# Window attention on one core: scores in four 64x64 tiles, stacks moved without a stop in DRAM, and half of the f16 rounding on VectorE

## The chip, the cores and the metric

The kernel runs on one core of one Trainium2 chip. The metric is the device time of one execution in microseconds. Three runs of the kernel before gave 507.66, 511.57 and 513.79 us; the median is 511.57 us.

## The reference, cut to what matters

```python
# x: (8, 32, 32, 256) f32
x = x + L0(gn(x))        # 16 heads of 16 channels, windows of 8x8 = 64 tokens
x = x + L1(gn(x))        # gn: 32 groups of 8 channels over all pixels of a sample

# L0, for each of 8*16 windows
qkv = part @ qkv_w.T + qkv_b
attn = (q * SCALE) @ k.T + bias_table[REL_IDX] + MASK   # (windows, 16, 64, 64)
out = softmax(attn) @ v
# L1: h = x @ W.T + b, then over the 8 samples as time, for each pixel and channel
v = v + (h_t - v) / 2 ;  s = (v >= 1) ;  v = v * (1 - s)
```

L1 has a threshold, so L0 must be exact to almost f32. The kernel reaches that with operands split into two f16 parts, a rounded one ("hi") and the rest ("lo"), and with three products for each (hi hi, lo hi, hi lo).

## The kernel before, in words

The work is tiled by rows of windows: 8 samples of 4 rows of 4 windows, 32 rows in all. A row is two **pairs** of windows, so that the main loop has 64 pairs, `n` = 0 to 63; a pair is "even" (first of its row) or "odd". Each engine has its own instruction stream, written out by hand, in this order for every pair; the engines meet only at semaphores. No scheduler or planner reorders anything.

TensorE (`pair` at line 1076, the helpers above it), in the odd pair of row r: projections of q and k for row r + 2 (L934 to L936, 24 products); in the even pair: the projection of v for row r + 1 (L944 to L946, 12 products). Then `scores(n)`: for each of the two banks of `score_ps`, eight pairs of a bias product (L1007, full array) and a score product (L1011, 96 rows by 128 columns), 64 columns each. Between the banks it transposes the maxima of this pair (L1029, `turn_maxima`). It holds the last of the score products until `max_rows_done` and until the stacks for the next pair have landed (`await_tile_operands`, L1087), and then subtracts the maxima with 16 products in 64x64 tiles (L1021). Then come `max_scores` of the next pair (L982, L991), the products with v of the pair before (L1045, 24) and two transposes of the finished attention of n - 2 (L1055).

The score product takes its three f16 terms from **stacks**: 96 partitions, in which q_hi, q_lo and k_hi, k_lo stand above each other in the right order. A head's 16 channels lie spread over partitions in `q_flat` and `k_flat`, so the stacks are made by DMA. SyncE issues all of that on one queue (`move_q_and_k`, L318): 3 stores of the flat tiles to DRAM (L303, L306), then 12 loads from there (L309, L314), 15 transfers a row. `k_stack` is 128 columns wide with zeros where the other head is, so its loads write pieces of 64 f16. There are two stacks each, used by turns.

ScalarE, for every pair: (odd) normalisation of row r + 3 (L481) and the rounded parts of q and k (L503); (even) `xn_hi` (L497) and the rounded v (L520); the transposed maxima (L599); then for each bank the exponential twice, once in f32 (`probs`, L608) and once rounded to f16 (`p_hi`, L609); and the bias of the attention (L572).

GpSimd: `p_lo = probs - p_hi` for each bank (L446, waits for `p_hi_done`), the addition of the attention to x (L432), `xn_lo` (L402) and once a sample the Newton steps of the norm (L225 to L233), whose result ScalarE needs for the normalisation (L481).

VectorE: the low parts of q, k (L758) and v (L777), the maxima (L783), statistics (L647), the division of the attention (L794, L798), and the small steps of the norm (L676 to L690).

Setup ahead of the loop splits the weights (L543, L732), scales the biases (L737, L739), and makes four variants of the position bias plus mask (L751, L528, L532, L418), the last two of them beside pairs 3 and 4. The spiking stage (L874 to L883, L923) comes after pair 63 and takes the last 70 us or so.

Of the kernel before, what the change touches and what calls it, by code (L numbers as in the profile page):

```python
# [6 lines left out]
def swin_attention_then_lif_kernel(nc, image, x, qkv_w, qkv_b, bias_table, lif_w, lif_b, out):  # L7
# [14 lines left out]
    ALU = mybir.AluOpType  # L22
# [25 lines left out]
    with ctx:  # L48
# [16 lines left out]
        both_parts = sb("both_parts", [128, 2, WS], f16)  # L65
        group_avg = sb("group_avg", [128, 128], f32)
        pick_max = sb("pick_max", [128, 2 * HALVES, 128], f16)
        bias_k = sb("bias_k", [128, 4, 2 * QUADS, 128], f16)
        bias_q = sb("bias_q", [128, 4, 2, HALVES, 128], f16)
# [24 lines left out]
        k_stack = [sb(f"k_stack{i}", [128, QUADS, HALVES * WCOLS, 128], f16) for i in range(2)]  # L94
        q_spill = [nc.dram_tensor(f"q_spill{i}", [2, 32, QUADS, HALVES * ROWTOK], f16).ap() for i in range(2)]
        k_spill = [[nc.dram_tensor(f"k_spill{i}{part}", [32, QUADS, HALVES * ROWTOK], f16).ap() for part in ("hi", "lo")] for i in range(2)]
# [26 lines left out]
        stack_cleared = sem("stack_cleared")  # L123
# [30 lines left out]
        q_spilled = sem("q_spilled")  # L154
        k_hi_spilled = sem("k_hi_spilled")
        k_lo_spilled = sem("k_lo_spilled")
# [8 lines left out]
        p_hi_done = sem("p_hi_done")  # L165
# [30 lines left out]
        def slot_total(row, y, per):  # L196

            return (row + (2 - y % 2)) * (per // 2)
# [57 lines left out]
        def w_columns(tile, first, c, h, ordered):  # L256

            cols = tile[:, c, first + h * 128:first + (h + 1) * 128]
            if first == 2 * C:
                return cols  # L260
            if ordered:
                return cols.rearrange("p (r g) -> p r g", g=QUADS)
            return cols.rearrange("p (g r) -> p r g", g=QUADS)
# [22 lines left out]
        def _(sp):  # L286
# [15 lines left out]
            def spill(flat, part, spilled, kept):  # L302
                sp.dma_start(kept.rearrange("r g n -> (r g) n"), flat[:, part, :]).then_inc(spilled, 16)  # L303

            def spill_q(slot):
                sp.dma_start(q_spill[slot].rearrange("t r g n -> (r g) t n"), q_flat[:, :, :]).then_inc(q_spilled, 16)  # L306

            def stack_q(slot, rows, kept):
                sp.dma_start(q_stack[slot][rows, :, :, :].rearrange("r g n i -> r (g n i)"), kept).then_inc(stacked[slot], 16)  # L309
# [327 lines left out]
        def _(dve):  # L637
# [182 lines left out]
            def pair(n, row, k, s):  # L820
# [11 lines left out]
                if not is_last_pair(n):  # L832
                    maxima(n + 1)
# [331 lines left out]
```

## Time and profile before

| | us |
|---|---|
| median of 3 runs | 511.57 |
| the profiled execution's own time | 516.01 |
| its span, first to last instruction | 514.3 |
| TensorE busy | 433.2 (84%) |
| VectorE busy | 408.8 (79%) |
| ScalarE busy | 380.1 (74%) |
| GpSimd busy | 274.8 (53%) |
| mean granted TensorE clock | 0.950 of full |
| DMA: packets, under 512 bytes | 136780, 107506 |

No engine is busy all the time; TensorE is nearest to it, but its busy time is that of modelled, pipelined matmuls. The chain that ended last gives 19% of the span to the queue of SyncE, 31% to TensorE, 13% to ScalarE and 11% to DMA.

### The profile page before, as it was taken

Reading aid. Unit: us, or ns where it says so; the run is one execution under the profiler, and the core shown is the slowest. Engines: PE = TensorE matmul, PEld = TensorE weight load, DVE = VectorE, ACT = ScalarE, POOL = GpSimd, SP = SyncE. Lnnn points to the kernel's source line nnn. Section 1 sums busy time; section 2 is a strip of 40 time slices with the busy share of each in tenths; the row PEclk is TensorE's granted clock in tenths of the full one; section 3 lists DMA queues with packets and bytes.
Section 4 is the critical chain, followed back from the end, with each engine's and each line's share of the span. In section 5 each row is a group of like instructions: output and inputs, shape, how many; then the busy total and the mean of one; then the engine's idle time right before and its main releaser. Section 6 shows DMA issues by size and latency. Waiting matters only on the chain.

```text
span 514.3 us, 19277 instructions
## 1 busy us (share of the span) xinstructions
PE 433.2 (84%) x7848; PEld 400.7 (78%) x7848; DVE 408.8 (79%) x872; ACT 380.1 (74%) x897; POOL 274.8 (53%) x380
## 2 busy tenths in 40 slices
PE   0477956998889879889988898989898987799996
PEld 0366856987889879789878797978798986588885
DVE  7957866798789859868888778879767887588887
ACT  6357776887889869779878787978788957745560
POOL 3534674567566746567666557556756648420000
PEclk9977977999999989989999989999999989889999
DMA  7145551465555563565555555554545450023333
GB/s 216 70 104 144 126 123 47 101 149 134 126 123 136 125 151 83 144 151 130 111 147 127 135 135 132 130 135 104 112 104 116 107 138 13 22 103 124 143 128 139
DMA packets 136780, 61.56 MB, mean 120 GB/s; under 512 B 107506, under 2 KB 125172, under 8 KB 136692
## 3 DMA queue, kind: packets, MB, share of 16 engines
q1 hardware_dynamic: 136352, 60.33, 46.5%
q8 instruction: 62, 1.02, 0.9%
q14 instruction: 26, 0.21, 0.1%
q10 hardware_dynamic: 340, 0.01, 0.0%
HBM read 35.13 MB, written 25.17 MB: 117 GB/s over the span
## 4 chain that ended last, share of the span: by engine, by line
PE 31%; SPq 19%; ACT 13%; DMA 11%; DVE 10%; issue 7%; POOL 7%; ACTq 0%; DVEq 0%; POOLq 0%
SPq L314 13%; DMA k_stack<-k_spill0lo 5%; SPq L309 4%; PE pv_ps L1045 3%; POOL p_lo L446 3%; PE score_ps L923 3%; ACT v_hi L520 3%; PE proj_ps L923 3%; PE pv_ps L923 3%; DMA k_stack<-k_spill1lo 2%; PE proj_ps L934 2%; PE score_ps L1021 2%; ACT k_flat L503 2%; PE max_ps L923 2%; PE proj_ps L935 2%
## 5 line engine op out<-in xcount | busy, mean ns | idle before, releaser
L446 POOL TENSOR_TENSOR p_lo<-probs,p_hi 128x512 f16<-128x512 f32 x128 | 146.4, 1165 | 132.7 <-ACT p_hi L609 78.9
L1011 PE MATMUL score_ps<-q_stack,k_stack 96*128 96x64 f16 x1024 | 86.6, 194 | 45.2 <-ACT max_rows L599 18.0
L1011 PEld LDWEIGHTS score_ps<-q_stack,k_stack 96*128 96x128 f16 x1024 | 71.9, 98 | 52.5 <-ACT max_rows L599 38.5
L608 ACT ACTIVATE probs<-score_ps 128x512 f32<-128x512 f32 x128 | 77.0, 602 | 46.9 <-PE score_ps L1021 43.4
L783 DVE TENSOR_REDUCE neg_max<-max_ps 128x16 f16<-128x1024 f32 x64 | 78.3, 1224 | 27.6 <-PE max_ps L991 26.6
L934 PE MATMUL proj_ps<-xn_hi,w_hi 128*128 128x256 f32 x256 | 78.6, 307 | 12.7 <-DVE w_lo L732 8.1
L1007 PE MATMUL score_ps<-both_parts,bias_k 128*128 128x64 f16 x1024 | 78.3, 194 | 0.0
L609 ACT ACTIVATE p_hi<-score_ps 128x512 f16<-128x512 f32 x128 | 77.4, 605 | 0.0
L777 DVE TENSOR_TENSOR v_lo<-proj_ps,v_hi 64x256 f16<-64x256 f32 x128 | 54.2, 424 | 28.4 <-ACT v_hi L520 26.8
L935 PE MATMUL proj_ps<-xn_lo,w_hi 128*128 128x256 f32 x256 | 74.1, 289 | 0.0
L936 PE MATMUL proj_ps<-xn_hi,w_lo 128*128 128x256 f32 x256 | 73.8, 288 | 0.0
L1007 PEld LDWEIGHTS score_ps<-both_parts,bias_k 128*128 128x128 f16 x1024 | 70.5, 99 | 2.7
L934 PEld LDWEIGHTS proj_ps<-xn_hi,w_hi 128*128 128x128 f32 x256 | 51.0, 199 | 16.6 <-DVE w_lo L732 8.1
L1045 PE MATMUL pv_ps<-v_hi,p_hi 128*128 128x68 f16 x512 | 57.7, 200 | 2.8 <-POOL p_lo L446 2.8
L520 ACT ACTIVATE v_hi<-proj_ps 64x256 f16<-64x256 f32 x128 | 50.4, 394 | 13.0 <-PE proj_ps L946 11.5
L1045 PE MATMUL pv_ps<-v_lo,p_hi 128*128 128x68 f16 x512 | 57.5, 198 | 0.0
L1045 PE MATMUL pv_ps<-v_hi,p_lo 128*128 128x68 f16 x512 | 57.3, 198 | 0.0
L798 DVE TENSOR_TENSOR attn<-pv_ps,recip 64x256 f32<-64x256 f32 x128 | 54.0, 422 | 3.0
L1045 PEld LDWEIGHTS pv_ps<-v_hi,p_hi 128*128 128x128 f16 x512 | 50.1, 102 | 8.0 <-POOL p_lo L446 3.4
L935 PEld LDWEIGHTS proj_ps<-xn_lo,w_hi 128*128 128x128 f32 x256 | 51.1, 199 | 0.0
L936 PEld LDWEIGHTS proj_ps<-xn_hi,w_lo 128*128 128x128 f32 x256 | 50.9, 199 | 0.0
L1045 PEld LDWEIGHTS pv_ps<-v_hi,p_lo 128*128 128x128 f16 x512 | 50.0, 100 | 0.0
(130 smaller groups left out, 1214.2 us busy)
## 6 DMA issues: line engine op xcount, KB each, us to landing
xc<-in_x_dram SPq DMA_DIRECT2D x32, 256.0 KB, 3.5
q_spill<-q_flat SPq DMA_DIRECT2D x32, 256.0 KB, 2.7
q_stack<-q_spill SPq DMA_DIRECT2D x32, 256.0 KB, 3.7
out_dram<-xc SPq DMA_DIRECT2D x32, 256.0 KB, 2.3
q_stack<-q_spill SPq DMA_DIRECT2D x32, 128.0 KB, 3.8
k_spill0hi<-k_flat SPq DMA_DIRECT2D x16, 128.0 KB, 2.2
k_spill0lo<-k_flat SPq DMA_DIRECT2D x16, 128.0 KB, 3.3
k_stack<-k_spill0hi SPq DMA_DIRECT2D x32, 64.0 KB, 3.1
```

The lines of the kernel that those rows point to most:

```text
L314: sp.dma_start(k_stack[slot][rows, quads, :, e * WS:(e + 1) * WS], k_spill[slot][part][e * D:(e + 1) * D, quads, :].rearrange("d g (n j) - ...
L446: pool.tensor_tensor(p_lo[p][:, quads, :, :].rearrange("p g w i -> p (g w i)"), probs[:, quads, :, :].rearrange("p g w i -> p (g w i)"), p ...
L520: last = act.activation(v_block(v_hi[slot], w, e), v_part(w, e), ACT.Copy)
L608: act.activation(probs[:, quads, :, :].rearrange("p g w i -> p (g w i)"), score_ps[:, h, :], ACT.Exp)
L609: act.activation(p_hi[p][:, quads, :, :].rearrange("p g w i -> p (g w i)"), score_ps[:, h, :], ACT.Exp)\
L783: dve.tensor_reduce(neg_max[:, :].rearrange("p (m n) -> p m n", m=2)[:, :, 0:8], max_ps[:, :, :].rearrange("p m (n j) -> p m n j", j=WS), ...
L934: pe.matmul(dst, w_hi[:, c, cols], high[:, tok], start=(c == 0), stop=False)
L935: pe.matmul(dst, w_hi[:, c, cols], low[:, tok], start=False, stop=False)
L936: last = pe.matmul(dst, w_lo[:, c, cols], high[:, tok], start=False, stop=(c == HALVES - 1))
L1007: pe.matmul(dst, bias_k[:, variant(k, w), h * QUADS + 2 * mid + q, :], both_parts[:, 0, :], start=(h == 0 and q == 0 and w == 0), stop=False)
L1011: pe.matmul(dst, k_stack[slot][0:96, 2 * mid + q, at, :], q_stack[slot][0:96, 2 * mid + q, at, :], start=False, stop=False)
L1045: last = pe.matmul(cols[:, :, g, :], pp[p][:, g // 2 * 4 + h * 2 + g % 2, :, :].rearrange("p w i -> p (w i)"), vv[k // 2][:, p, h * QUADS ...
```

## The change

Four things are done together.

1. **Scores.** The score products and the bias products go in four 64x64 tiles of the array. The stacks are 48 partitions high and come twice, at partitions 0 and 64; `k_stack` has no zeros and is half as wide. For a pair there are now 32 score products of 64 columns (L1007 of the new kernel) and 8 bias products of 512 columns (L1016) in place of 16 and 16 on the full array; `max_scores` has 4 bias products of 512 and 32 tile products of 64 columns in place of 8 of 256 and 16 of 128; the transpose of the maxima becomes 4 products in tiles, written in f32. Both banks are now begun only after ScalarE has read both banks of the pair before (`exp_done`), and the maxima are turned ahead of the products, not between the banks. The wait for the next stacks stands ahead of `max_scores`.
2. **Stacks.** They are filled straight from `q_flat` and `k_flat`, 12 transfers a row with 64 KB each in pieces of 1 KB, and none through DRAM. All 12 wait for `score_ps_done` of the odd pair that frees the slot. The four writers of the flat tiles (L503 on ScalarE, L758 on VectorE in the kernel before) now wait until all 12 transfers of the row before have landed (`await_moved`).
3. **Rounding.** For the first bank ScalarE computes the exponential once; VectorE rounds it to f16 after the maxima (L832), and GpSimd's first `p_lo` waits for that.
4. **Setup.** No clearing of the stacks; the scaling of the biases goes ahead of the norm's first roots; the weights are put in another order of columns; the bias variants are written in eight smaller steps on ScalarE and four on GpSimd.

```diff
             def move_q_and_k(slot, r):
 
-                sp.wait_ge(k_hi_done, r + 1)
-                spill(k_flat, HI, k_hi_spilled, k_spill[slot][0])
-                sp.wait_ge(k_lo_done, r + 1)
-                spill_q(slot)
+                sp.wait_ge(q_flat_done, r + 1)
                 if not is_first(r, 2):
                     sp.wait_ge(score_ps_done, 4 * (r - 2) + 4)
-                spill(k_flat, LO, k_lo_spilled, k_spill[slot][1])
-                sp.wait_ge(k_hi_spilled, (r + 1) * 16)
-                stack_k(slot, 0, 0, slice(0, QUADS))
-                stack_k(slot, 32, 0, slice(0, 2))
-                stack_k(slot, 64, 0, slice(2, QUADS))
-                sp.wait_ge(q_spilled, (r + 1) * 16)
...
+                stack(slot, q_stack, 0, q_flat, HI)
+                stack(slot, q_stack, 2, q_flat, HI)
+                sp.wait_ge(k_hi_done, r + 1)
+                stack(slot, k_stack, 0, k_flat, HI)
+                stack(slot, k_stack, 1, k_flat, HI)
+                sp.wait_ge(q_lo_done, r + 1)
+                stack(slot, q_stack, 1, q_flat, LO)
+                sp.wait_ge(k_lo_done, r + 1)
+                stack(slot, k_stack, 2, k_flat, LO)
...
+            def stack(slot, stacks, term, flat, part):
+                for r in range(2):
+                    first = r * WS + term * D
+                    sp.dma_start(stacks[slot][first:first + D, :, :, :].rearrange("d g n i -> d g (n i)"),
+                                 flat[r * WS:(r + 1) * WS, part, :])\
                       .then_inc(stacked[slot], 16)
...
+        def await_moved(eng, r):
+
+            if r > 0:
+                eng.wait_ge(stacked[(r - 1) % 2], stacked_total(r - 1))
...
             def q_high(done):
                 act.wait_ge(q_ps_done, done)
-                wait(act, q_spilled, 16 * (done - 1))
+                await_moved(act, done - 1)
                 with_bias(q_flat, 0).then_inc(q_flat_done, 1)
...
-                    act.activation(probs[:, quads, :, :].rearrange("p g w i -> p (g w i)"), score_ps[:, h, :], ACT.Exp)
-                    act.activation(p_hi[p][:, quads, :, :].rearrange("p g w i -> p (g w i)"), score_ps[:, h, :], ACT.Exp)\
-                       .then_inc(p_hi_done, 1)
+                    last = act.activation(probs[:, quads, :, :].rearrange("p g w i -> p (g w i)"), score_ps[:, h, :], ACT.Exp)
+                    if h == 1:
+                        last = act.activation(p_hi[p][:, quads, :, :].rearrange("p g w i -> p (g w i)"), score_ps[:, h, :], ACT.Exp)
+                    last.then_inc(exp_done, 1)
...
                 if not is_last_pair(n):
                     maxima(n + 1)
+                wait(dve, pv_ps_done, n - 1)
+                dve.wait_ge(exp_done, n * 2 + 1)
+                dve.tensor_copy(p_hi[p][:, 0:QUADS, :, :].rearrange("p g w i -> p (g w i)"),
+                                probs[:, 0:QUADS, :, :].rearrange("p g w i -> p (g w i)")).then_inc(p_hi_copied, 1)
...
+            def scores(n, row, k):
 
                 slot, p = k // 2 % 2, k % 2
...
+                for g, w in itertools.product(range(QUADS), range(2)):
+                    col = (2 * g + w) * WS
+                    for h, e in itertools.product(range(HALVES), range(2)):
+                        at = h * WCOLS + 2 * p + w
+                        rows = stacks_of[e ^ h]
+                        pe.matmul(score_ps[halves[e], h, col:col + WS], k_stack[slot][rows, g, at, :], q_stack[slot][rows, g, at, :],
+                                  start=(g == 0 and w == 0), stop=False)
...
+                        pe.matmul(score_ps[halves[e], h, :].rearrange("p (g w i) -> p g w i", g=QUADS, w=2), flip[rows, :], biases,
+                                  start=False, stop=False)
+                pe.wait_ge(max_rows_done, n + 1)
...
-                scores(n, row, k, await_tile_operands)
+                wait(pe, exp_done, n * 2)
+                turn_maxima(n)
+                scores(n, row, k)
...
                 if not is_last_pair(n):
+                    await_max_operands(*following)
                     max_scores(following[2])
```

How the change moves instructions, at three places. First TensorE, around `scores` of pair 0: the end of it before (-; fifteen more pairs of L1007 and L1011 stand ahead), and all of it now (+), with `max_scores` of pair 0 ahead and of pair 1 behind.

```order
-L1011 MATMUL score_ps<-q_stack,k_stack 128x64
-L1021 MATMUL score_ps<-max_rows,pick_max 64x2x64 x16
-L982 MATMUL max_ps<-bias_q,ident_h 64x256 x8
-L991 MATMUL max_ps<-k_stack,q_stack 64x128 x16
+L987 MATMUL max_ps<-bias_q,ident_h 64x512 x4
+L994 MATMUL max_ps<-k_stack,q_stack 64x64 x32
+L1033 MATMUL max_ps<-ident_h,neg_max 64x64 x4
+L1007 MATMUL score_ps<-q_stack,k_stack 64x64 x32
+L1016 MATMUL score_ps<-bias_s,flip 64x512 x8
+L1023 MATMUL score_ps<-max_rows,pick_max 64x2x64 x16
+L987 MATMUL max_ps<-bias_q,ident_h 64x512 x4
+L994 MATMUL max_ps<-k_stack,q_stack 64x64 x32
```

The turn of the maxima (L1033) now stands ahead of all score products, and nothing but the 16 products L1023 stands behind the wait for ScalarE's `max_rows`.

Second, SyncE's queue, the transfers of one row. Before:

```order
L303 DMA k_spill1hi<-k_flat 128x512 [waits k_hi_done]
L306 DMA q_spill<-q_flat 128x2x512 [waits k_lo_done]
L303 DMA k_spill1lo<-k_flat 128x512 [waits score_ps_done]
L314 DMA k_stack<-k_spill1hi 16x32x64 [waits k_hi_spilled]
L314 DMA k_stack<-k_spill1hi 16x32x64
L314 DMA k_stack<-k_spill1hi 16x16x64 x4
L309 DMA q_stack<-q_spill 64x2048 [waits q_spilled]
L309 DMA q_stack<-q_spill 32x2048
L314 DMA k_stack<-k_spill1lo 16x16x64 [waits k_lo_spilled]
L314 DMA k_stack<-k_spill1lo 16x16x64 x3
```

And now:

```order
L310 DMA q_stack<-q_flat 16x4x512 [waits score_ps_done,q_flat_done]
L310 DMA q_stack<-q_flat 16x4x512 x3
L310 DMA k_stack<-k_flat 16x4x512 [waits k_hi_done]
L310 DMA k_stack<-k_flat 16x4x512 x3
L310 DMA q_stack<-q_flat 16x4x512 [waits q_lo_done]
L310 DMA q_stack<-q_flat 16x4x512
L310 DMA k_stack<-k_flat 16x4x512 [waits k_lo_done]
L310 DMA k_stack<-k_flat 16x4x512
```

Fifteen transfers in two steps have become twelve in one, but the first of them now waits for `score_ps_done`, which before only the third did.

Third, VectorE in a plain even pair and the odd one behind it, now; before, the two CAST rows were not there and the rest was the same.

```order
L779 TENSOR_REDUCE neg_max<-max_ps 128x2x8
L832 CAST p_hi<-probs 128x512
L790 RECIPROCAL recip<-pv_ps 128x32
L794 TENSOR_TENSOR attn<-pv_ps,recip 64x256 x2
L641 BN_STATS x_stats<-xc 128x6 x2
L754 SCALAR_TENSOR_TENSOR q_flat<-proj_ps,b_cols,q_flat 128x256 x2
L754 SCALAR_TENSOR_TENSOR k_flat<-proj_ps,b_cols,k_flat 128x256 x2
L779 TENSOR_REDUCE neg_max<-max_ps 128x2x8
L832 CAST p_hi<-probs 128x512
L641 BN_STATS x_stats<-xc 128x6 x2
```

The rounding stands right behind the maxima of the next pair, and whatever VectorE does after it comes later by its length.

## Rows read from the trace of the kernel before

**Rows 1.** Waits over the whole execution: engine, line, releaser; us, times, longest.
```profile
PE score_ps L1011 <- DMA k_stack<-k_spill0lo: 15.2, 11, 2.0
PE score_ps L1011 <- DMA k_stack<-k_spill1lo: 9.9, 8, 2.7
ACT xn L481 <- POOL shift L233: 8.8, 7, 1.4
```

**Rows 2.** Chain that ended last, in order of time: start, length, what.
```profile
225.26 0.21 PE proj_ps L944
...
231.07 0.12 PE proj_ps L934
```

**Rows 3.** Windows of 1 us: busy by engine (instructions), clock, DMA share, GB/s.
```profile
187.00:188.00 1.00, 1.00 (x6) 1.00 (x6) 1.00 (x4) 1.00 (x4) 1.00 (x1) 0.50 0.33 52
```

**Rows 4.** ScalarE in order of time: start, length, line, operation, count [idle before].
```profile
98.47 0.28 ACT L599 ACTIVATE max_rows<-max_ps 128x128 f16<-128x128 f16 x1
...
228.64 0.28 ACT L599 ACTIVATE max_rows<-max_ps 128x128 f16<-128x128 f16 x1
...
234.11 0.84 ACT L503 ACTIVATE k_flat<-proj_ps,b_cols 128x256 f16<-128x256 f32 x2
234.84 0.28 ACT L599 ACTIVATE max_rows<-max_ps 128x128 f16<-128x128 f16 x1
235.84 0.60 ACT L608 ACTIVATE probs<-score_ps 128x512 f32<-128x512 f32 x1 [0.72 <-PE score_ps L1021]
236.33 0.59 ACT L609 ACTIVATE p_hi<-score_ps 128x512 f16<-128x512 f32 x1
...
239.60 0.28 ACT L599 ACTIVATE max_rows<-max_ps 128x128 f16<-128x128 f16 x1
...
243.65 0.87 ACT L503 ACTIVATE q_flat<-proj_ps,b_cols 128x256 f16<-128x256 f32 x2
...
415.31 0.28 ACT L599 ACTIVATE max_rows<-max_ps 128x128 f16<-128x128 f16 x1
```

**Rows 5.** TensorE in order of time, from the last score product to max_scores.
```profile
228.97 0.20 PE L1011 MATMUL score_ps<-q_stack,k_stack 96*128 96x64 f16 x1
229.10 0.42 PE L1021 MATMUL score_ps<-max_rows,pick_max 64*64 64x128 f16 x16
229.35 0.39 PE L982 MATMUL max_ps<-bias_q,ident_h 64*64 64x256 f16 x8
229.57 0.39 PE L991 MATMUL max_ps<-k_stack,q_stack 64*64 64x128 f16 x16
```

**Rows 6.** SyncE's queue in order of time.
```profile
236.82 3.39 SPq L314 DMA_DIRECT2D k_stack<-k_spill0hi  x6
...
256.34 0.92 SPq L347 DMA_DIRECT2D xc<-in_x_dram  x2
```

**Rows 7.** DMA issues of the page: count, KB each, median us from issue to landing.
```profile
k_spill1hi<-k_flat SPq DMA_DIRECT2D x16, 128.0 KB, 1.7
...
k_stack<-k_spill1lo SPq DMA_DIRECT2D x64, 32.0 KB, 3.1
```

**Rows 8.** VectorE in order of time, setup and one odd pair.
```profile
10.20 0.86 DVE L724 COPY pick_max<-ident_h 64x512 f16<-64x512 f16 x2
...
13.90 4.17 DVE L732 SCALAR_TENSOR_TENSOR w_lo<-w_raw,w_hi 128x128 fp32r<-128x128 f32 x12
17.99 5.02 DVE L737 TENSOR_SCALAR b_cols<-b_cols 128x2 f32<-128x2 f32 x1
...
236.22 1.23 DVE L783 TENSOR_REDUCE neg_max<-max_ps 128x16 f16<-128x1024 f32 x1 [0.36 <-PE max_ps L991]
```

**Rows 9.** GpSimd in order of time, setup.
```profile
20.09 2.89 POOL L382 MEMSET v_lo<- 128x1088 f16 x3
```

**Rows 10.** Chain that ended last, setup and last pairs.
```profile
26.31 0.58 PE proj_ps L944
...
439.93 2.28 POOL p_lo L446 x2
```

More of the change, by code:

```diff
@@ L640, in _ @@
             dve.memset(three_halves[:, :], 1.5)
-            for slot in range(2):
-                dve.memset(q_stack[slot][96:128, 2:QUADS, :, :].rearrange("r g n i -> r (g n i)").bitcast(f32), 0.0)
             dve.memset(masks[:, :, :], 0.0).then_inc(setup_dve, 1)
@@ L985, in max_scores @@
-                for w in range(2):
-                    for h in range(HALVES):
-                        col = (2 * w + h) * 128
-                        at = h * WCOLS + 2 * (k % 2) + w
-                        for mid, rows in enumerate(halves):
-                            for q, queries in enumerate(halves):
-                                last = pe.matmul(max_ps[queries, mid, col:col + 128], q_stack[slot][rows, 2 * mid + q, at, :],
-                                                 k_stack[slot][rows, 2 * mid + q, at, :],
-                                                 start=False, stop=(w == 1 and h == 1))
+                first, last_variant = variant(k, 0), variant(k, 1)
@@ new lines, in scores @@
+                pe.wait_ge(max_rows_done, n + 1)
+                for w, m in itertools.product(range(2), range(2)):
+                    for h, e in itertools.product(range(HALVES), range(2)):
+                        rows = halves[e ^ h]
+                        dst = score_ps[halves[e], h, :].rearrange("p (m q w i) -> p m w q i", m=2, q=2, w=2)[:, m, w, :, :]
+                        last = pe.matmul(dst, pick_max[rows, (2 * w + m) * 2 + h, :],
+                                         max_rows[p][rows, :].rearrange("p (q i) -> p q i", q=2),
+                                         start=False, stop=(w == 1 and m == 1))
+                        if w == 1 and m == 1 and e == 1:
+                            last.then_inc(score_ps_done, 1)
@@ L1027, in turn_maxima @@
             def turn_maxima(n):
                 pe.wait_ge(neg_max_done, n + 1)
-                pe.transpose(max_ps[:, 0, :].bitcast(f16)[:, 0:128], neg_max[:, :], ident_h[:, :])\
-                  .then_inc(max_turned, 1)
+                for q, queries in enumerate(halves):
+                    for rows in halves:
+                        last = pe.matmul(max_ps[rows, q, 0:WS], neg_max[queries, rows], ident_h[queries, queries], start=True, stop=True)
+                last.then_inc(max_turned, 1)
```

202 lines of the change are left out of this document (88 added, 114 removed).

## Prediction

> **What bounds the kernel now.** I read the table of waits first, since no engine is busy all the time. TensorE waits 25.1 us (15.2 + 9.9, 19 times) for the transfers that fill the stacks [rows 1]; nothing else that a transfer does holds an engine so long. Then the chain that ended last, which says what a wait costs behind it: after a long one, v's projection runs at 0.21 us a product [rows 2], because the granted clock is 0.50, the lower of the two levels, 1.2 GHz, for some 3.5 us [rows 3]; undisturbed it takes 0.12 us [rows 2]. Then ScalarE in order of time, because its `max_rows` comes once a pair and marks the beat. From pair 7 to pair 59 it beats from 98.47 to 415.31 us [rows 4], 26 rows of windows in 316.84 us, 12.19 us a row. Where no transfer is late, a row takes 10.96 us: 6.20 from the even pair to the odd (228.64 to 234.84), 4.76 from there to the next (to 239.60) [rows 4]. So the stacks cost about 1 us a row, and the rest is a beat in which TensorE and ScalarE hand work to each other.
>
> **The sum**, against the profiled execution's own 516.0 us.
>
> *Stack waits.* The stacks no longer go through DRAM: one landing (1.7 to 3.1 us [rows 7]) and three issues fewer. I take all 25.1 us of waits away, but give back 0.26 us for each of the 19, the gap in which TensorE waits for `max_rows` anyway (4.9 us), and add four stretches at half clock, 12 v products each, at 0.09 us (0.21 - 0.12 [rows 2]), 1.1 us: 4.3. That is **-24.5**.
>
> *TensorE's products.* The tile products before pass at 16 of 128 columns in 0.22 us and 8 of 256 in 0.22 us (229.35 to 229.57, and as much again) [rows 5], so four tiles work at once. The 32 products of 64 columns then take 0.22 us if columns set the pace and at most 0.44 if every instruction costs what L991's do. `max_scores` goes from 0.44 to 0.43 to 0.65 us and stands on the path; I take +0.1. In `scores` 1 us of full-array work becomes 0.22 to 0.44 + 0.43 us (8 of 512 columns at twice L982's time), but that is hidden: from the end of k's projection (234.11) ScalarE still needs to 235.12 for `k_flat` and `max_rows` [rows 4]. What stood on the path there is the last score product ahead of L1021, 0.13 us (228.97 to 229.10 [rows 5]), and it goes. Over 62 pairs (0.1 - 0.13): **-2**. The Trainium skill (TensorEngine Tiling (Array Packing), Performance Considerations, Instruction Overhead) speaks against small tiles: each matmul has about 60 cycles of overhead, so that few columns save nothing. By that rule 64 columns are just long enough to be worth issuing, and the sum would stay as it is; no row here has a product of 64 columns in a tile.
>
> *ScalarE's exponential.* One of four goes; the step from one to the next is 0.49 us (235.84 to 236.33 [rows 4]), 31 us in all. I count **0**: k's rounding at 234.11 begins when TensorE's projection ends, and the v rounding of the even pair likewise, so ScalarE would wait there instead.
>
> *VectorE's rounding.* 64 new casts of 512 elements. COPY of 512 took 0.43 us each (0.86 for 2 [rows 8]); at the pace of L783, 1.23 us for 1024 [rows 8], it would be about 0.7. I take 0.43, since the form is nearest. It stands behind the maxima, 0.38 + 1.14 us after the exponentials start (236.22 against 235.84, and its length [rows 4, 8]), so GpSimd's first `p_lo` starts 2.0 us after them, where it now can at 1.2: 0.8 us later. Mostly hidden: TensorE wants `p_lo` only after the next `scores`, 4.8 us on. Not hidden where GpSimd is the chain: seven times, once a sample, ScalarE waits 8.8 us in all for its roots [rows 1], and 0.85 more each is **+6**. And in the last pairs, with no projection left to cover, `p_lo` is on the chain that ended last [rows 10]: three times 0.8, **+2.5**.
>
> *The new wait `await_moved`.* Twelve issues at 0.46 us (0.92 for two [rows 6]), the last landing 2.2 us after its issue (between 1.7 and 3.1 [rows 7]), begun 0.1 us after the odd pair's score products: the move ends 7.8 us after them. The next `q_flat` starts 7.81 us after the exponentials in a fast row (243.65 against 235.84 [rows 4]). So it just fits. Behind it VectorE gets tight: busy 79% of the span, about 9.6 of 12.19 us a row, it will have 10.5 of some 11.5. What both give back by coming late now and then I put at 0.2 us for 29 rows, an estimate: **+5**. Bounds for the move: 12 x 0.46 + 1.7 = 7.2 us, which costs nothing, and 12 x 0.57 (3.39 for six [rows 6]) + 3.1 = 10 us, which is rival A.
>
> *Setup.* `b_cols` stands 5.02 us on VectorE [rows 8], while GpSimd clears v (its memsets run to 22.98 [rows 9]), and v's projection starts only at 26.31 [rows 10]. Now that scaling comes before GpSimd is busy, and v can follow k's projection at 23.2: **-3**. It is -3 only if the bias sum L751 that moves up isn't held by the same memsets; L732, with two inputs as well, ended at 18.07 [rows 8] with the first three memsets under way (17.2, as the other three start at 20.09 [rows 9]). If it is held, 0. The Trainium skill agrees (SBUF — State Buffer, SBUF: two separate sides): VectorE and GpSimd share a pair of ports under a lock, and an operation with two SBUF inputs meets it only against a GpSimd operation that reads SBUF. The bias variants are written in more and smaller steps: **+2**.
>
> Sum: -24.5 - 2 + 0 + 6 + 2.5 + 5 - 3 + 2 = **-14**, 502 us against 516.0. The median of the runs lies 4.4 us under the profiled execution; late transfers are what differs from one to the next, and these are what goes, so I give half of that: **499.5 us**, 2.4% under the median. 1% of the median (506.5 to 516.7) is about what a measurement can tell from no change.
>
> **Rivals.**
>
> A. *The queue becomes the loop* (slower). If the moves take 0.57 us an issue and 3.1 to land, they end 10 us after the odd scores; then comes what is left of a fast row behind `q_flat`, 10.96 - 7.81 = 3.15 us, so a row takes 13.2 us, 1.0 over today's 12.19: 29 us on 516, less 3 to 5 of setup and of the runs' median, about **540**. It decides from a move of 9.0 us on. For it: all 12 transfers now wait for the odd scores, and ScalarE itself waits for their landing, which it did not. Against it: the pieces are of 1 KB, where 107506 of 136780 packets were under 512 bytes, and the 0.57 us belong to transfers cut into the smallest. 9%.
>
> B. *The tiles run two at a time, not four* (slower). `score_ps` bank 0 is now written by both halves of rows, partitions 0 to 63 from one and 64 to 127 from the other; before, each bank had one row half. At half rate the bias and score products take 0.86 + 0.44 to 0.88 us and the 16 of L1021 (0.25 us [rows 5]) twice that: 0.25 + about 0.45 beyond ScalarE's cover of 1.0 us, 0.7 x 62 = 43 us more, about **542**. The Trainium skill has such a rule (TensorEngine Tiling (Array Packing), Restrictions and Gotchas, PSUM Pressure): different row tiles cannot access the same PSUM bank simultaneously. Against it: no partition of a bank is written from two row halves at a time. 6%.
>
> C. *VectorE fills the row* (no change). With casts of 0.7 us, now and then held by an operation of GpSimd, it has 11.0 to 11.2 us of work in 11.5 and cannot catch up behind a wait; it gives back 0.4 us more a row: 499.5 + 12, **511**. 18%.
>
> D. *The freed time is used* (faster). ScalarE's half microsecond shortens the step from odd to even, and the last transfers' jitter is gone: 10.7 us a row where I count on 11.5, half of that in the 26 rows: **489**. 12%.
>
> E. The stacks come too late again from somewhere else, so that the change does not do what it says, and the time stays at 512. 3%.
>
> My forecast has the rest, 52%, with 491 to 508 as its own range. With D, most of C and E the range is **486 to 518**; A, B and the edges lie outside. Faster by over 1%: 0.60 (most of the forecast, and D); within 1%: 0.24 (its upper end, C and E); slower: 0.16 (A, B).
>
> **What would show it.** TensorE's waits for `k_stack` and `q_stack` near nothing, and no stretch at clock 0.50 in the main loop. `max_rows` 11.0 to 11.5 us a row, and one row a sample near 13, ScalarE waiting 2 us for GpSimd's roots there. 32 products of 64 columns in 0.2 to 0.45 us. The cast at 0.43 us, GpSimd's first `p_lo` 2 us behind the exponentials. ScalarE's `q_flat` with little or no wait for a transfer: waits of 1 us there are rival A. v's first projection at 23 us and not at 26.31. I am wrong if rows stay at 12 us with the stack waits gone; then the loop has closed over another engine, and VectorE's idle time in a row says whether it is C.

## The result and the profile after

| | median us | runs | ratio to before | span of the profile | clock |
|---|---|---|---|---|---|
| before, beside it | 511.87 | 4 (507.66 to 513.79) | 1 | 514.3 | |
| changed | 565.15 | 4 (562.96 to 566.6) | 1.105 [1.0972, 1.1127] | 563.1 | 0.915 |

The change makes the kernel 10.5% slower; I had forecast 499.5 us and a range of 486 to 518. The page of the changed kernel: busy time and share, DMA, and the chain that ended last by engine.

```profile
span 563.1 us, 22270 instructions
PE 432.4 (77%) x9320; PEld 368.5 (65%) x9320; DVE 431.6 (77%) x936; ACT 354.3 (63%) x849; POOL 282.3 (50%) x392
DMA packets 42488, 44.98 MB, mean 80 GB/s; under 512 B 8082, under 2 KB 33940, under 8 KB 42388
SPq 31%; PE 21%; ACT 13%; DMA 11%; DVE 9%; POOL 7%; issue 7%; ACTq 0%; DVEq 0%; POOLq 0%
```

TensorE has as much work as before, in a longer span. There is a third as many packets, and yet SyncE's queue has grown from 19% of the chain to 31%. The waits of the changed kernel (engine, line, releaser: us, times, longest):

```profile
POOL p_lo L439 <- DVE p_hi L832: 181.7, 55, 6.3
PEld score_ps L1023 <- ACT max_rows L594: 117.1, 63, 6.7
ACT q_flat L500 <- DMA k_stack<-k_flat: 56.8, 25, 4.4
DVE q_flat L754 <- ACT q_flat L500: 45.0, 25, 3.7
ACT xn L478 <- POOL shift L233: 18.0, 7, 3.5
```

TensorE's 25.1 us of waits for the stacks [rows 1] are gone, as forecast: no wait of TensorE for a transfer is left. ScalarE now waits 56.8 us for the transfers that fill the stacks, 25 times, ahead of `q_flat`; and its seven waits for the roots grew from 8.8 us [rows 1] to 18.0. The beat, which answers to [rows 4] (ScalarE: start, length, instruction [idle before]):

```profile
102.64 0.29 ACT L594 ACTIVATE max_rows<-max_ps 128x128 f16<-128x128 f32 x1
...
243.64 1.09 ACT L603 ACTIVATE probs<-score_ps 128x512 f32<-128x512 f32 x2 [0.81 <-PE score_ps L1023]
...
254.50 0.84 ACT L500 ACTIVATE q_flat<-proj_ps,b_cols 128x256 f16<-128x256 f32 x2 [1.04 <-DMA k_stack<-k_flat]
...
256.43 0.29 ACT L594 ACTIVATE max_rows<-max_ps 128x128 f16<-128x128 f32 x1
257.31 1.08 ACT L603 ACTIVATE probs<-score_ps 128x512 f32<-128x512 f32 x2 [0.59 <-PE score_ps L1023]
...
462.20 0.29 ACT L594 ACTIVATE max_rows<-max_ps 128x128 f16<-128x128 f32 x1
```

Pair 7 to pair 59 takes 359.56 us, 13.83 a row against 12.19. These 26 rows hold 42.7 of the 48.8 us between the two spans. The rest: first `max_rows` 1.1 us earlier (42.12 against 43.24), from there to pair 7 5.3 more, from pair 59 to the last pair 2.9 more, and after it 1.0 less. Why a row takes 13.8 us is in the chain of waits from one odd pair's scores to the next row's `q_flat` (start, length, what):

```profile
242.88 0.70 PE score_ps L1023 x16
...
243.64 0.55 SPq L310
...
246.14 1.54 SPq L310
...
247.72 0.59 SPq L310
...
250.91 0.60 SPq L310
...
251.55 2.86 DMA k_stack<-k_flat
...
254.50 0.10 ACT q_flat L500
```

The scores end at 243.58, eleven issues at 251.51, and the twelfth, begun at 251.55, has landed at 254.41 (2.86 us from its issue). Then `q_flat`, k's flat, `max_rows` and the next odd scores follow, to 257.25, and SyncE starts again at 257.31. This is a closed ring of 13.67 us: odd scores, twelve issues one behind the other, landing, `q_flat`, odd scores. Each step waits for the one before it. It closes in the mean of the 26 rows too: 0.13 us to the first issue, 8.21 from there to the start of the twelfth, 2.79 to `q_flat`, 2.71 to the end of the next odd scores, together the 13.83 of the row.

TensorE is idle for most of the time ahead of the odd scores, and behind that its granted clock is at the lower of its two levels, 1.2 GHz (window: busy by engine with instructions, clock, DMA share, GB/s). In the ring this costs some 0.2 us: the 16 products of the odd scores take 0.70 us at 242.88 and 0.47 in the next row.

```profile
241.00:243.00 2.00, 0.12 (x8) 0.12 (x11) 1.18 (x3) 1.83 (x6) 1.25 (x2) 0.80 0.00 0
243.00:248.00 5.00, 5.00 (x87) 4.69 (x88) 3.89 (x9) 2.72 (x6) 1.86 (x2) 0.50 0.18 56
```

### The profile page after: what moved, and what is told of

It is laid out like the page before. It is cut to its first block, busy times and chain, and to the rows that moved or that the text cites. A ratio compares the mean times of both kernels' runs of the same rounds, so it can differ in the third digit from the quotient of the medians.

```text
span 563.1 us, 22270 instructions
## 1 busy us (share of the span) xinstructions
PE 432.4 (77%) x9320; PEld 368.5 (65%) x9320; DVE 431.6 (77%) x936; ACT 354.3 (63%) x849; POOL 282.3 (50%) x392
## 4 chain that ended last, share of the span: by engine, by line
SPq 31%; PE 21%; ACT 13%; DMA 11%; DVE 9%; POOL 7%; issue 7%; ACTq 0%; DVEq 0%; POOLq 0%
SPq L310 30%; DMA k_stack<-k_flat 10%; ACT k_flat L500 3%; ACT q_flat L500 3%; ACT xn L478 3%; PE score_ps L1023 3%; PE proj_ps L923 2%; PE pv_ps L923 2%; PE score_ps L923 2%; POOL p_lo L439 2%; PE max_ps L923 2%; PE pv_ps L1049 2%; ACT v_hi L517 2%; POOL xn_lo L391 2%; ACT max_rows L594 1%
## 5 line engine op out<-in xcount | busy, mean ns | idle before, releaser
L1023 PE MATMUL score_ps<-max_rows,pick_max 64*64 64x128 f16 x1024 | 28.7, 234 | 86.4 <-ACT max_rows L594 86.3
L1023 PEld LDWEIGHTS score_ps<-max_rows,pick_max 64*64 64x64 f16 x1024 | 17.8, 112 | 117.3 <-ACT max_rows L594 117.1
L934 PE MATMUL proj_ps<-xn_hi,w_hi 128*128 128x256 f32 x256 | 77.7, 303 | 18.0 <-POOL xn_lo L391 13.8
L603 ACT ACTIVATE probs<-score_ps 128x512 f32<-128x512 f32 x128 | 69.7, 595 | 26.7 <-PE score_ps L1023 20.4
L1049 PE MATMUL pv_ps<-v_hi,p_hi 128*128 128x68 f16 x512 | 63.7, 208 | 5.1 <-POOL p_lo L439 4.8
L500 ACT ACTIVATE q_flat<-proj_ps,b_cols 128x256 f16<-128x256 f32 x64 | 26.8, 469 | 64.0 <-DMA k_stack<-k_flat 56.8
L1049 PE MATMUL pv_ps<-v_lo,p_hi 128*128 128x68 f16 x512 | 63.8, 207 | 0.0
L1049 PE MATMUL pv_ps<-v_hi,p_lo 128*128 128x68 f16 x512 | 63.7, 207 | 0.0
L754 DVE SCALAR_TENSOR_TENSOR q_flat<-proj_ps,b_cols,q_flat 128x256 f16<-128x256 f32 x64 | 28.0, 479 | 45.2 <-ACT q_flat L500 45.0
L567 ACT ACTIVATE attn_cm<-proj_ps,b_cols 128x128 f32<-128x128 f32 x128 | 40.4, 371 | 22.7 <-PE proj_ps L1059 22.7
L1049 PEld LDWEIGHTS pv_ps<-v_lo,p_hi 128*128 128x128 f16 x512 | 53.0, 107 | 0.3
```

What stands on the lines that cost most here:

```text
L500: last = act.activation(flat[:, HI, tok], proj_ps[:, first // 2, tok], ACT.Identity, bias=b_cols[:, first + h:first + h + 1])
L603: last = act.activation(probs[:, quads, :, :].rearrange("p g w i -> p (g w i)"), score_ps[:, h, :], ACT.Exp)
L934: pe.matmul(dst, w_hi[:, c, cols], high[:, tok], start=(c == 0), stop=False)
L1023: last = pe.matmul(dst, pick_max[rows, (2 * w + m) * 2 + h, :], max_rows[p][rows, :].rearrange("p (q i) -> p q i", q=2), start=False, stop ...
L1049: last = pe.matmul(cols[:, :, g, :], pp[p][:, h * QUADS + g, :, :].rearrange("p w i -> p (w i)"), vv[k // 2][:, p, h * QUADS + g, :, :, :] ...
```

## The experiments

Ratios are to the kernel before, measured beside each, with 95% intervals. "e5", in the second group, is the version that beats both kernels.

| | kernel | median us | ratio |
|---|---|---|---|
| e1 | changed, two flat tiles | 519.75 | 1.0138 [1.0079, 1.0197] |
| e2 | changed, three slots | 526.82 | 1.0271 [1.0204, 1.0338] |
| e3 | changed, both | 517.59 | 1.0107 [1.0076, 1.0138] |
| e4 | changed, ScalarE rounds | 563.35 | 1.0945 [1.0845, 1.1045] |
| e5 | e3, ScalarE rounds | 487.41 | 0.9643 [0.9557, 0.9729] |
| e6 | before, VectorE rounds | 531.64 | 1.0417 [1.0141, 1.0694] |
| e7 | e3, rounding ahead of the maxima | 498.42 | 0.987 [0.9792, 0.9947] |
| e8 | changed, 14 transfers | 607.63 | 1.2008 [1.192, 1.2096] |
| e9 | before, three slots | 512.54 | 0.9951 [0.9913, 0.9989] |
| e10 | e5 without the third slot | 496.9 | 0.9656 [0.9584, 0.9728] |
| e11 | e5 without the second flat tiles | 513.76 | 0.9982 [0.9938, 1.0025] |
| e12 | e5, seven single transfers in three rows | 527.99, one run | |
| e13 | e5 and an idle rounding | 511.65 | 1.0005 [0.9959, 1.0052] |
| e14 | e5, xn_hi behind max_rows | 502.47 | 0.9818 [0.9754, 0.9882] |
| e15 | e5 again | 485.53 | 0.9493 [0.9435, 0.9551] |
| e16 | e5, VectorE's wait alone | 486.74 | 0.9508 [0.9412, 0.9603] |
| e17 | e16 and 0.52 us of load | 488.96 | 0.9542 [0.9468, 0.9616] |
| e18 | e17 and p_lo held by it | 519.98 | 1.0148 [1.0064, 1.0231] |

### The ring: e1, e2, e3, e8

The ring has two edges that buffers can cut: q_flat waits for the landing (a second flat tile), and the first issue waits for the odd scores (a third slot).

```diff
-        q_flat = sb("q_flat", [128, 2, HALVES * ROWTOK], f16)
+        q_flat = [sb(f"q_flat{i}", [128, 2, HALVES * ROWTOK], f16) for i in range(2)]   # e1, e3; k_flat alike
...
-                await_moved(act, done - 1)
+                await_moved(act, done - 2)
...
-                    sp.wait_ge(score_ps_done, 4 * (r - 2) + 4)
+                    sp.wait_ge(score_ps_done, 4 * (r - 3) + 4)                          # e2, e3; slots row % 3
```

> The changed kernel with two flat tiles each for q and k, used by turns, so that their writers wait for the move of two rows back and not for the last one. Theory R (a ring of the queue: odd scores, 12 issues of 0.63 us, landing, the wait before q's rounding, next odd scores): the waits of ScalarE for a transfer (56.8 us over 25 rows) go, the row falls from 13.8 to some 11.2 us, and the time to about 500 us. Theory V (VectorE's rounding makes p_lo late, GpSimd waits 181.7 us for it, and that sets the row): nothing changes, 560 us or more. Theory T (the products in tiles and the clock are what costs): 560 us too.

> The changed kernel with three stacks each and not two, so that a move no longer waits for the odd pair's scores; the wait of the flat tiles' writers for the last move stays. Theory R: the move starts when q's rounded part is there, about 2.5 us earlier, and the ring closes over q's rounding alone: 12 issues, landing, q's rounding, 10.9 us or a little more; row near 11.5, time 505 to 515 us. Theories V and T: 560 us.

> Both of the edits before in one. Theory R: no ring is left, only the queue's own load of 12 issues a row (8.3 us of 11): as e1 or a few us less, 490 to 500 us. If the queue's load itself were the bound it would stay near e1. Theories V and T: 560 us.

Cutting either edge takes 38 to 45 us away, both 47.6. That is nearly all of the loss of 53.3 us, and it is the ring. With one edge cut something is left at the other: in e1 TensorE's products wait 2.7 us for the stacks (its weight loads, at the same places, 4.3), in e2 `q_flat` on ScalarE waits 28.6 us; in e3 no engine waits for a stack's transfer. But all three are 12 to 20 us slower than I had expected from the ring alone, and e3 still isn't faster than before. The group on the rounding looks for that rest.

e8 lengthens the ring instead:

```diff
+                for r2 in range(2):
+                    sp.dma_start(spare[r2 * D:(r2 + 1) * D, :, :], q_flat[r2 * WS:(r2 + 1) * WS, HI, :]).then_inc(stacked[slot], 16)
```

> The changed kernel with two more transfers of the same shape per row, to a spare tile that nobody reads (14 instead of 12 in the move). Theory R (the ring: exponential, q_flat, issues one after the other, landing of the last, next q_flat): each row pays 2 x 0.63 = 1.26 us, 26 to 29 rows, 565 goes to 597 to 602. Rival (the landing and bandwidth, not the issue, sets the ring): the last landing shifts by less, 565 to 580.

The time goes up 42 us, the row from 13.83 to 15.19. That is 1.36 us for two transfers, 0.68 each: the median issue (0.59 + 0.04) and a little more, as nearly every move has a long issue in it (below). It is somewhat above the 597 to 602 expected; the direction and the size fit the ring.

### The rounding: e4 to e7

```diff
-                    if h == 1:
+                    if True:                      # ScalarE rounds both banks: e4 on the changed kernel, e5 on e3
                         last = act.activation(p_hi[p][:, quads, :, :]..., ACT.Exp)
...
-                dve.wait_ge(exp_done, n * 2 + 1)
-                dve.tensor_copy(p_hi[p][:, 0:QUADS, :, :]..., probs[:, 0:QUADS, :, :]...).then_inc(p_hi_copied, 1)
```

> The changed kernel with ScalarE taking the exponential of the first bank twice again, and no rounding on VectorE. Theory R: ScalarE has waits to spare in the ring, so nothing but the once-a-sample wait for GpSimd's roots gets shorter, 0.8 us seven times: 555 to 562 us. Theory V: the loss goes, 515 us or less.

> Two q_flat/k_flat tiles and three slots as in e3, and ScalarE rounds both banks again. Theory G (with the ring gone, the rounding on VectorE is what is left: it starts behind the maxima of the next pair, so the GpSimd subtraction p_lo, the xn_lo behind it and project_q come about 1 us later in each row, and 1.7 us later in the rows with the roots): row 12.20 goes to about 11.6 and the time to 498 to 504. Rival S (SyncE's twelve issues at 0.62 us, 7.4 us of queue in each row plus their landing, are what is left, and ScalarE gets its 0.60 us a pair back on the path): 515 to 530.

Within the ring it makes no difference who rounds (e4, 563.35 against 565.15), since the rest waits for the queue anyway. With the ring open it makes 30 us (e3 517.59, e5 487.41), more than the 14 to 20 that I had expected. Whoever had tried e4 alone would have acquitted the rounding.

e6 adds VectorE's rounding to the kernel before, e7 moves it ahead of the maxima in e3:

> The kernel before with one thing of the change: VectorE rounds the first bank, behind the maxima, and ScalarE only the second. Prices part three alone. Theory G: GpSimd's chain is as late here as in e3, so 517 to 526. Rival (the delay is hidden behind the 9.4 us waits for the stacks through the spill): 508 to 514. My prediction put +8.5 on the rounding and nothing back from ScalarE: 520.

> e3 with VectorE's rounding put ahead of the maxima of the next pair (in the trace of e3 the exponential of the first bank ends at 241.4 and the rounding starts at 243.02, behind the 1.23 us reduction). Theory G: p_lo starts 1 us earlier, row 12.20 to 11.8 or so, 505 to 512. Rival M: the maxima come 0.4 us later or wait for the exponential, the turn and the next scores with them, and what GpSimd gains TensorE loses: 516 to 525.

e6: +4.2%, some 18 us, with a wide interval (its four runs took 523.8 to 533.5 us); three of the four lie above the 517 to 526 of theory G. e7: 498.42, 19 us below e3 and 11 above e5, below what either side expected. So the place of the rounding in VectorE's order is most of its price. The chain of e3 in one row shows the way it takes (start, length, what):

```profile
239.35 1.11 POOL p_lo L439
240.46 0.69 POOL xc L422
241.15 1.24 POOL xn_lo L391
...
242.44 0.39 PE proj_ps L934
...
245.57 0.84 ACT k_flat L500 x2
...
246.63 0.42 PE score_ps L1023 x16
247.05 0.22 PE max_ps L987 x4
247.26 0.24 PE max_ps L994 x29
```

GpSimd runs `p_lo`, the residual's sum and `xn_lo` without a gap, and q's projection starts when `xn_lo` is done. In e5 `xn_lo` ends 0.5 us ahead of q's projection (GpSimd, then TensorE, in order of time):

```profile
225.83 2.29 POOL L436 TENSOR_TENSOR p_lo<-probs,p_hi 128x512 f16<-128x512 f32 x2 [2.90 <-PE pv_ps L1042]
228.08 0.73 POOL L422 TENSOR_TENSOR xc<-xc,attn_cm 128x256 f32<-128x256 f32 x1
228.76 1.28 POOL L391 TENSOR_TENSOR xn_lo<-xn,xn_hi 128x512 fp32r<-128x512 f32 x1
```

```profile
230.54 0.36 PE L927 MATMUL proj_ps<-xn_hi,w_hi 128*128 128x256 f32 x1
```

So I had the right engine and the wrong cover. I had counted on TensorE wanting `p_lo` 4.8 us later; what matters in this row is `xn_lo`, two places behind `p_lo` in GpSimd's queue. In the rows with roots it is the Newton steps, which stand behind `xn_lo` and which ScalarE's normalisation waits for, in e3 (first row) and in e5:

```profile
ACT xn L478 <- POOL shift L233: 23.0, 7, 3.5
```

```profile
ACT xn L475 <- POOL shift L233: 7.0, 6, 1.3
```

### What of the rounding costs: e13, e16, e17, e18

> e5 with VectorE's rounding added at the place it has in the change (behind the maxima), into a spare tile that nobody reads; ScalarE rounds both banks too, and GpSimd waits for ScalarE. Theory G (what costs is that the subtraction p_lo waits for VectorE): 487 to 493, VectorE's 0.43 us a pair is absorbed. Rival L (VectorE's load, or its hold on GpSimd while it rounds, is what costs): 500 to 518, as in e3.

e13 gave 511.65, as if VectorE's load cost 26 us. But its rounding isn't the change's. In e3 (first row) GpSimd waits for it; in e13 (the other two, VectorE and GpSimd) it meets `p_lo`:

```profile
243.02 0.43 DVE L832 CAST p_hi<-probs 128x512 f16<-128x512 f32 x1
```

```profile
292.64 1.38 DVE L832 CAST spare<-probs 128x512 f16<-128x512 f32 x1
...
291.44 2.30 POOL L437 TENSOR_TENSOR p_lo<-probs,p_hi 128x512 f16<-128x512 f32 x2 [0.73 <-ACT p_hi L605]
```

0.43 us alone, 1.38 beside `p_lo`; the median of e13's 63 is 1.10 us, where the changed kernel's 64 have 0.43, and VectorE is busy 88% of the span. The Trainium skill (SBUF — State Buffer, SBUF: two separate sides) has such a rule: a VectorE operation in a two-port mode or with two SBUF inputs and a GpSimd operation share one pair of ports under an exclusive lock, and who comes second waits for the whole instruction of the other. The trace agrees: the rounding starts at 292.64 while the second `p_lo` runs, until 293.74, and ends 0.28 us behind it; 61 of the 63 end 0.2 to 0.35 us behind the GpSimd instruction in which they began. No row says in which mode the rounding runs. How the 26 us divide between VectorE's longer time and operations of GpSimd held by it wasn't tried. The next three leave that out, with a reduction from one source:

```diff
+                dve.wait_ge(exp_done, n * 2 + 1)                                                       # e16, e17, e18
+                dve.tensor_reduce(spare[:, :], w_hi[:, 0, 0:352].bitcast(f32), AX.X, ALU.max)          # e17, e18 (.then_inc(p_hi_copied, 1))
...
+                        pool.wait_ge(p_hi_copied, n + 1)                                               # e18, ahead of the first p_lo
```

> e5, and VectorE waits behind the maxima for the first bank's exponential, with no instruction of its own. Theory G (the lateness of p_lo costs): 485 to 489. Rival W (VectorE's queue held for the exponential costs): 495 or more.

> e16 with a reduction of 352 constants per partition behind the wait, about 0.43 us of VectorE in each pair, that shares nothing with GpSimd. Theory G: 487 to 494. Rival L (VectorE's load): 500 or more.

> e17 with GpSimd's first p_lo held until that reduction is done, as the change holds it for the rounding; ScalarE still rounds both banks. Theory G: the step from e17 to here is most of the 30 us, 508 to 520. Rival: within 5 us of e17, and what is left is ScalarE's order in the change.

486.7, 489.0, 520.0. VectorE's wait costs nothing that can be measured (e15, e5 again, is 485.5), its load 2 us (the reduction takes 0.515 us, a little more than the rounding's 0.43), and `p_lo` held until VectorE is through 31 us. e18's row is 12.18 us, e3's 12.20. This settles it: the lateness of `p_lo` is the price, and the load is not. Most of it is paid in few rows: from pair 7 to pair 59 e18 takes 26.0 us longer than e17, 17.9 of them in the six rows with roots (15.2 us each against 12.2), the other 8.1 in twenty rows.

### What is left, and why the direct move pays: e9 to e12, e14, e15

> The kernel before, moves through DRAM and all, with nothing changed but a third slot for both stacks and for the spill, so that a row's move starts a row earlier. Theory B (the 24.5 us of waits for the stacks are a matter of buffers, and the direct move is not needed to be rid of them): 485 to 500, and of the 26 us that e5 gains on the kernel before the direct move and the tiles hold little. Rival D (the gain of e5 is the direct move's and the tiles'): 505 to 514.

Theory B is refuted: 0.5% is all that a third slot gives the kernel before (its third slot found room only once two tiles of the last stage were laid over the bias table). 21.9 of the 25.1 us of waits for the stacks stay. SyncE in e9, and the wait that TensorE has for the move before:

```profile
230.78 0.63 SPq L303 DMA_DIRECT2D k_spill1hi<-k_flat  x1
...
233.22 3.36 SPq L314 DMA_DIRECT2D k_stack<-k_spill1hi  x6
236.62 1.85 SPq L309 DMA_DIRECT2D q_stack<-q_spill  x2
238.52 1.90 SPq L314 DMA_DIRECT2D k_stack<-k_spill1lo  x4
243.31 0.34 SPq L303 DMA_DIRECT2D k_spill2hi<-k_flat  x1
```

```profile
232.56 0.19 PE L1012 MATMUL score_ps<-q_stack,k_stack 96*128 96x64 f16 x1 [1.62 <-DMA k_stack<-k_spill0lo]
```

The move starts with k's flat and not with a free slot, its last issue ends 9.6 us later, and a landing comes on top (in the median row of e9 it is 12.2 us from the first issue to the last landing): the way through DRAM is by itself as long as the row that it has, 12.07 us. The direct move is shorter (10.77 us in the row above, 243.64 to 254.41). That this is what it buys, once it may overlap the row, is argued from these lengths; no run has the direct move without the tiles.

```diff
# e10 = e5 without three slots, e11 = e5 without two flat tiles, e5's rounding in both
```

> e5 without the third slot: two q_flat/k_flat tiles, ScalarE rounds both banks. Theory R (the ring has two edges, odd scores to the first issue and last landing to q_flat; cutting either opens it): within 1% of e5, 487 to 493. Rival (the third slot is what starts the move early enough, and the second flat tile only shifts the wait to TensorE): 500 to 520.

> e5 without the second flat tiles: three slots, ScalarE rounds both banks. Theory R: the ring is cut at its other edge, but q_flat still waits for a landing; the move takes 10.8 us of a row of 10.8 to 11.2 us, so it is just too long: 495 to 510. Rival: as good as e5, 487 to 492.

The second flat tile is the edge to cut: 0.9656, where e5 had 0.9643. In microseconds it is 496.9 against 487.4, outside the 487 to 493 expected, in a row of 11.77 us against 11.22; and in e10 TensorE's products still wait 7.6 us for the stacks, ten times, where in e5 none does. So the third slot may be worth a few us on top; the ratios don't settle it. The third slot alone leaves `q_flat` waiting for landings, 26.3 us in 20 waits, a row of 12.22 us: the time of before, 0.9982, worse than I expected of theory R.

```diff
+                    for dst, what in ((spare[0:64, 0, :], src[0:64]), (spare[:, 0, :], src), (spare[0:32, :, :], src), (spare_dram, src), ...):
+                        sp.dma_start(dst, what).then_inc(spare_sem, 16)
+                        sp.wait_ge(spare_sem, 16 * spare_count[0])
```

> e5 with seven single transfers behind the moves of rows 4, 12 and 20, each waited for before the next: 64x1 KB to 64 partitions, 128x1 KB to 128 partitions, 128x1 KB to 32 partitions of 4 KB, 128x1 KB to DRAM, 16x1 KB, 64x1 KB to 16 partitions of 4 KB (the shape of the stacks' moves), 128x256 B. Theory I (an issue's time goes with its rows): 64x1 KB 0.59 us in either layout, 128 rows 1.0 or more, 16 rows below 0.4. Rival (a fixed price per transfer inside the chip's memory, lower to DRAM: 0.46 us in the spills of the kernel before): 0.59 for all of them but the one to DRAM, 0.46. The time itself tells nothing here, SyncE waits on purpose.

SyncE's issues behind the move of row 4, in the order of the expectation (start, length); from issue to landing they took 1.93, 2.03, 2.76, 1.78, 1.81, 2.37 and 2.05 us by the chain:

```profile
95.20 0.51 SPq L342 DMA_DIRECT2D spare<-w_hi  x1
97.14 0.51 SPq L342 DMA_DIRECT2D spare<-w_hi  x1
99.19 0.60 SPq L342 DMA_DIRECT2D spare<-w_hi  x1
101.97 0.34 SPq L342 DMA_DIRECT2D spare_dram<-w_hi  x1
103.77 0.60 SPq L342 DMA_DIRECT2D spare<-w_hi  x1
105.60 0.59 SPq L342 DMA_DIRECT2D spare<-w_hi  x1
107.99 0.51 SPq L342 DMA_DIRECT2D spare<-w_hi  x1
```

Neither theory holds. Among these seven an issue doesn't go with rows or bytes: 16 rows of 1 KB 0.60, 128 rows 0.51. It goes with where it writes: DRAM 0.34, SBUF over 64 or 128 partitions 0.50 to 0.51, over 16 or 32 partitions 0.58 to 0.61, and so again in rows 12 and 20. The stacks' moves are of the dearest kind. (This one execution took 527.99 us, which says nothing: SyncE waits for each landing.) But that is no rule for all transfers. In the kernel before, by the medians of their places in the row, the loads from DRAM into 16 partitions of `k_stack` take 0.55 and 0.63 us with 64 KB, and with 32 KB 0.42 to 0.45 in seven places and 0.62 in one; two stores of one shape to DRAM take 0.338 and 0.466. So the destination isn't all, and e12 doesn't say what else there is.

```diff
-                    xn_high(k // 2 % 2, row + 3)        # ahead of max_rows
+                    xn_high(k // 2 % 2, row + 3)        # behind it
```

> e5 with xn_hi put behind the copy of the maxima (max_rows) on ScalarE instead of ahead of it. In e5's chain of waits, from 226.53 on, attn_cm 0.65, xn_hi 0.52 and half of v_hi 0.63 stand between the exponentials and max_rows at 228.37. Theory A (ScalarE's order sets the even beat): 0.5 us less in each row, 26 to 29 rows, 473 to 479. Rival X (xn_lo and project_q, 0.7 us later than now, take it back in the odd beat): 484 to 490.

Refuted: 502.47, 17 us slower than e5 beside it (e15) and slower than the rival said as well. The step from odd to even stays at 4.6 us, and the step from even to odd goes from 6.18 to 6.7 us; `xn_lo` has no more than 0.5 us to spare, as above.

> e5 unchanged, beside e13 and e14 on one chip: 485 to 490, and a ratio to the kernel before of 0.96.

485.53 and 0.9493, the other time 487.41 and 0.9643: e5 is 3.6 to 5.1% faster than before, and 14% faster than the changed kernel.

## Why the prediction was wrong

**The step that failed is "The new wait `await_moved`"**, forecast at +5 us, measured at 45.4 with that wait moved back a row alone (e1) and at 47.6 with the third slot too (e3). The mechanism stood there, with its threshold (rival A, from a move of 9.0 us on). The term that was mis-sized is the move, and in it the issues:

- The issue: 0.46 us taken, 0.594 the median of the 384 issues in the trace after, 0.04 between two, and in 30 of the 32 moves one of 1.0 to 1.8 us, as at 246.14. From the first issue's start to the twelfth's it is 8.21 us in the mean row (7.91 in the row shown), where I had 5.5 for all twelve.
- The landing: 2.2 taken, from the last issue; 2.86 in the row shown, and 2.79 in the mean row from the twelfth issue's start to `q_flat`, 2.45 in the median one. This was nearly right.
- So the move ends 10.8 us after the odd scores in the row shown, and in the mean row `q_flat` starts 11.1 us after them, not 7.8. "It just fits" had no margin, and a step that just fits was to be priced at its upper bound.

A better price was in the trace of before. I took the issue of the x loads, because their pieces are large. Of the issues that fill these same stacks, those of `q_stack` and the 64 KB loads of `k_stack` cost more, and most 32 KB loads of `k_stack` a little less (line, count: min/median/max ns; the third row is of 32 KB loads alone, the second mixes both sizes):

```profile
L309 SPq DMA_DIRECT2D q_stack<-q_spill x64: 489/583/1961, 31.5 to 421.9; - x64
L314 SPq DMA_DIRECT2D k_stack<-k_spill0hi x96: 447/553/1810, 28.0 to 409.3; - x96
L314 SPq DMA_DIRECT2D k_stack<-k_spill0lo x64: 417/448/1559, 32.7 to 413.5; - x64
```

With 0.583 + 0.04 an issue and the 2.2 us of the forecast, added up as I had added them, the move is 9.7 us long, beyond the 9.0 at which rival A decides; with the landing counted from the last issue's start, as [rows 7] count it, 9.1, at the threshold. I gave rival A 9% and 540 us: 10 us and 3.15 behind it, a row of 13.2 where 13.83 came. What I held against it, that only transfers cut small take 0.57 us, e12 refutes (0.59 to 0.60 with pieces of 1 KB).

**VectorE's rounding**: +8.5 forecast. In the changed kernel it costs nothing (e4). On e5 it costs 30 us and on the kernel before 18. Its own time was right (0.43 us), and so was that GpSimd's chain carries it in the rows with roots. But I had 0.85 us for each of these, and it is 2.9 to 3.0 (in e3 15.1 us, in e5 12.2, in e18 15.2, in e17 12.2): 18 of the 26 us between e17 and e18. "Mostly hidden" in the other rows was wrong too, by 0.4 us a row. That the last pairs pay 2.5 us fits (2.5 in the last row, e3 against e5 and e18 against e17).

**ScalarE's exponential**: 0 forecast, 0 found in the ring (e4). Outside it, e18 has both exponentials and the late `p_lo` and is 2.4 us above e3, which has one fewer; the load of e18 is 0.09 us longer as well, so hardly anything is left for the exponential.

**The stack waits**: -24.5 forecast. TensorE's waits went completely. With ring and rounding out of the way e5 fits the sum of this term, the products and the setup: they come to -27.5, and e5 is 18 to 26 us faster than before by one measurement (by ratio and by medians) and 26 to 29 by the other. Which of the three terms gave it isn't shown: what the tiles give apart from the direct move was not tried.

**The products**: `max_scores` takes 0.22 + 0.25 us with 64 columns (the row of e3 above is cut off at 29 of the 32 products) where [rows 5] had 0.22 + 0.22, within the bounds 0.43 to 0.65 and at their low end. Four tiles do work at once. Rival B is out too: the 16 products of L1023, in which both row halves write to one bank, take 0.42 us, as those of L1021 did with a bank each [rows 5]. The rule that I had named beside it (the Trainium skill, TensorEngine Tiling (Array Packing), Restrictions and Gotchas, PSUM Pressure) shows no cost here.

**Setup**: -3 and +2 forecast; v's projection starts at 24.30, where it had been 26.31 and I had 23, and the first `max_rows` comes 1.1 us earlier.

**Rival C** (VectorE fills the row) is out: VectorE is busy 77% here, its 64 roundings take 0.43 us in the median and 0.61 at most, and e17 prices such a load at 2 us. D is what e5 reaches, by another road. Of the signs I had named, "waits of 1 us at `q_flat` are rival A" was the one that spoke.

## What to carry to other kernels

When a transfer goes from "off the path" to "waited for before the buffer is written again", draw the ring: who starts the move, how many issues follow each other on the queue, the last landing, who waits, and back. Price every issue at the dearest row of an issue that writes the same destination, and at its upper end if it just fits, and cut the ring with a second buffer at the writer (here one more q_flat and k_flat). When an operation moves to another engine, ask what stands behind its consumer in that engine's queue, in the rare rows as well: the load itself, 0.52 us a pair, cost 2 us here, what started late because of it 31, more than half of that in the few rows with roots. And an experiment inside a closed ring (e4) tells nothing of a cost outside it.

## What the hardware showed unexpectedly

- Among the seven shapes of e12 the time to issue a transfer from SyncE goes with the destination and not with rows or bytes: 0.34 us to DRAM, 0.50 to 0.51 to 64 or 128 partitions, 0.58 to 0.61 to 16 or 32. The 32 KB loads from DRAM in the kernel before don't keep to that (0.448 us into 16 partitions). Single issues take 1.0 to 2.2 us (one in 30 of the 32 moves of the changed kernel; the longest of e5 2215 ns).
- A rounding of 512 elements on VectorE takes 0.43 us alone and up to 1.40 beside GpSimd's subtraction (e13); this load, unlike that of e17, is dear, 26 us for 64 of them. What of this is VectorE's and what GpSimd's isn't shown.
- 32 products of 64 columns in four tiles pass in 0.25 us, 16 of 128 took 0.22 [rows 5]: so small a product costs its columns and hardly more.
